# Two head groups per output bank, a rebuilt opening, another order of the steps and 118 dummy matmuls in a one-core transformer block

## The chip, the cores and the metric

The kernel runs on one core of a Trainium2 chip. The metric is the device time of one execution in microseconds (us); of several runs the median counts. The engines are named as in the profile: PE is TensorE, DVE is VectorE, ACT is ScalarE, POOL is GpSimd, SP issues DMAs.

## What is computed

`x` is 4 x 512 x 128 in fp32. It is normalised to `xn`, and the result is `x + local(xn) + ffn(xn)`. Cut to what matters:

```python
# local: attention in chunks of 16 tokens, once on neighbours, once on every third token; 16 heads of 8
local = linear(chunk_attention(xn, 16) + dilated_chunk_attention(xn, 16, 3), Wo, bo)

# ffn: causal attention over all 512 tokens, 16 heads, low-rank q, k, v and rotary parts
probs = softmax(where(causal, qq @ kk.T / sqrt(8), min))
y     = (probs @ v).reshape(B, S, 128) @ W_o
x     = xn + y
# then a shared expert and two of seven routed experts
h     = silu(xt @ Wg) * (xt @ Wu) @ Wd          # for each of 8
out   = x + shared + sum(weight_e * routed_e)
```

## The kernel before

The host only lays out data; everything else is one program for one core. Activations of a batch (512 tokens) are turned so that features lie on partitions. The program is a list of steps, `ORDER`, which every engine walks in the same order, each doing its own part of a step; engines meet only on semaphores. So a step's place in the list sets its place in every queue, SP's and POOL's too. The fields after a step's name are the batch, then the head group or unit.

**Steps.** The opening of a batch is `XT` (transposes of the normalised tokens: L1211), `LK`, `LQ`, `LV` (local projections: L1216, L1300), `MA` and `MB` (projections for the causal attention and their rotated forms: L1221), `MV` (its values: L1227), and `STATS`, `LN` (normalisation on VectorE). `WF` (L1200) multiplies low-rank weights, once. VectorE adds the rotary parts (L961, L992, L993, L995, L965) and splits q and k into bf16 terms, and SP writes the terms to the stacks in which the score products find them (steps `ST`, `to_stack`, L484). `KD` spreads k over `k_diag` for the local attention (L774 on ScalarE, L1003 on VectorE).

`S.b.n` are products of the causal attention whose maxima VectorE takes (L1159 on TensorE, L1012 on VectorE, banks A); `SHIFT` turns a group's maxima and SP writes them back into the q stack. `E` are the same products again, shifted by the maxima (L1180, banks B), of which ScalarE takes the exponent (L830). A `*` in `ORDER` stands for the next S with the E that lies two head groups behind; their matmuls alternate on TensorE. 176 of each run in all. `mask` adds the causal triangles (L1166).

`PV.b.g.j` multiplies probabilities of head group `g` and key tile `j` with values and a column of ones (L1276) into one bank, `bank_c`: each head of the group has 32 of its 128 partitions, of which 9 are used. After the last `j` ScalarE copies the bank to `oT_mla` (L839). `Y.b.g` transposes it back (four transposes, L1283), and VectorE divides by the sums (L1074, L1075) into `y_mla`. The next group's first PV waits for the copy:

```python
if j == 0 and n > 1:
    pe.wait_ge(c_drained, (n - 1) // NT)
...
first = (HD + 1) * (4 * g + m)
```

`YT` and `X1` finish the causal attention. `LS`, `LR`, `PT`, `LO`, `LT`, `LW` are the local attention (L1318; L1026 and L1029 on VectorE). `R2`, `R3`, `X2T`, `ROUTE`, `PICK` are the second normalisation and the routing. The last part of the list are 32 experts (4 batches by 8): `GU` (gate and up, L1372, banks B) and `DOWN` (L1378, banks A). The expert weights take the room of `k_diag`, so they come behind the last `LS`.

**Banks.** Eight PSUM banks: rings A (2; S, LS, DOWN), B (3; E, GU) and M (2; everything else), and `bank_c`. `wait_free` makes TensorE wait until the bank's last user was read. In a pair of S and E it waits for both banks before the first matmul of the pair.

**Dummies.** `WARM` gives steps a number of fp32 matmuls of the identity with itself into `bank_c`, issued ahead of the step's waits: 6 ahead of `WF`, 2 ahead of `XT.0.1`, 2 ahead of `MA.0.0`, 10 ahead of `S.0.0`, one ahead of each of `S.0.2` to `S.0.11` (L1192).

## Time and profile before

| | us |
|---|---|
| median of 3 timed runs | 378.18 |
| lowest and highest of them | 376.24, 379.63 |
| the profiled execution | 371.83 |
| its span, first to last instruction | 369.6 |
| PE, DVE, ACT, POOL busy | 334.2, 285.0, 222.3, 123.0 |

The profile is one execution. Busy times are sums over instructions; matmuls are pipelined and their ends modelled, so that PE may be listed as busy while the next matmul could already stream in. The name behind an arrow (`<-`) is what released a waiting engine. The granted clock is 1.00 at full speed and 0.50 at half. The profiled execution is shorter than each of the timed runs.

### The profile page before, as it was taken

Reading aid. Unit: us, or ns where it says so; the run is one execution under the profiler, and the core shown is the slowest. Engines: PE = TensorE matmul, PEld = TensorE weight load, DVE = VectorE, ACT = ScalarE, POOL = GpSimd, SP = SyncE. Lnnn points to the kernel's source line nnn. Section 1 sums busy time; section 2 is a strip of 40 time slices with the busy share of each in tenths; the row PEclk is TensorE's granted clock in tenths of the full one; section 3 lists DMA queues with packets and bytes.
Section 4 is the critical chain, followed back from the end, with each engine's and each line's share of the span. In section 5 each row is a group of like instructions: output and inputs, shape, how many; then the busy total and the mean of one; then the engine's idle time right before and its main releaser. Section 6 shows DMA issues by size and latency. Waiting matters only on the chain.

```text
span 369.6 us, 11664 instructions
## 1 busy us (share of the span) xinstructions
PE 334.2 (90%) x4504; PEld 206.3 (56%) x4504; DVE 285.0 (77%) x720; ACT 222.3 (60%) x545; POOL 123.0 (33%) x148
## 2 busy tenths in 40 slices
PE   5779997898998989999989899888999999999994
PEld 5455664455564555565654565534546666656663
DVE  5979789799877988898998988987334577766743
ACT  5266345577675656677674766665765656456563
POOL 6186507040600826603312200000203563444443
PEclk9999999999999989999998999989999999999998
DMA  8435352222242123250222321106000000000000
GB/s 200 77 108 173 71 167 62 67 62 42 40 162 46 36 66 51 78 184 25 43 53 50 65 65 34 36 3 172 5 0 0 3 27 2 4 28 2 29 0 28
DMA packets 29141, 21.84 MB, mean 59 GB/s; under 512 B 12312, under 2 KB 26008, under 8 KB 29048
## 3 DMA queue, kind: packets, MB, share of 16 engines
q1 hardware_dynamic: 28872, 20.91, 22.8%
q8 instruction: 36, 0.59, 0.7%
q10 hardware_dynamic: 216, 0.20, 0.2%
q14 instruction: 17, 0.14, 0.1%
HBM read 6.81 MB, written 6.19 MB: 35 GB/s over the span
## 4 chain that ended last, share of the span: by engine, by line
PE 60%; DVE 28%; issue 5%; ACT 3%; DMA 3%; SPq 1%; POOL 0%; DVEq 0%; ACTq 0%; POOLq 0%
PE bank_B L1372 13%; DVE neg_max L1012 9%; PE bank_B L1180 8%; PE bank_c L1276 7%; PE bank_A L1378 7%; PE bank_A L1318 3%; PE bank_M L1283 2%; PE bank_B L1166 2%; DVE s_loc L1029 2%; DVE row_max L1026 2%; PE bank_M L1341 2%; PE bank_M L1221 2%; PE bank_c L1192 2%; PE bank_M L1211 1%; PE bank_M L1326 1%
## 5 line engine op out<-in xcount | busy, mean ns | idle before, releaser
L830 ACT ACTIVATE p_mla<-bank_B 128x512 f32<-128x512 f32 (+1 forms) x176 | 92.0, 561 | 54.6 <-PE bank_B L1166 31.0
L1012 DVE TENSOR_REDUCE neg_max<-bank_A 128x1 f32<-128x512 f32 (+3 forms) x176 | 106.9, 636 | 15.8 <-PE bank_A L1166 13.0
L1180 PE MATMUL bank_B<-q_stack,k_stack 54*128 54x512 bf16 (+3 forms) x256 | 62.4, 306 | 12.1 <-DVE neg_max L1012 8.2
L1159 PE MATMUL bank_A<-k_stack,q_stack 52*128 52x512 bf16 (+3 forms) x256 | 63.1, 307 | 3.2 <-DMA q_stack<-parts 2.2
L1372 PE MATMUL bank_B<-xrT,k_diag 128*128 128x512 f32 x128 | 60.9, 597 | 1.1 <-DVE k_diag L1137 1.1
L703 POOL TENSOR_TENSOR x<-x,q_part 128x512 f32<-128x512 f32 x31 | 39.5, 1274 | 58.0 <-ACT q_part L864 41.7
L1276 PE MATMUL bank_c<-p_mla,v_mla 128*32 128x384 f32 (+12 forms) x512 | 47.6, 453 | 0.4 <-ACT p_mla L830 0.4
L1180 PEld LDWEIGHTS bank_B<-q_stack,k_stack 54*128 54x128 bf16 x256 | 19.4, 94 | 49.6 <-issue 23.4
L864 ACT ACTIVATE q_part<-bank_A,expert_w 128x128 f32<-128x128 f32 x108 | 30.8, 369 | 24.6 <-PE bank_A L1378 24.6
L1137 DVE SCALAR_TENSOR_TENSOR k_diag<-k_diag,bank_B 128x512 f32<-128x512 f32 x32 | 22.0, 687 | 29.1 <-ACT k_diag L848 26.7
L1166 PE MATMUL bank_A<-masks 64*128 64x64 bf16 (+2 forms) x352 | 43.9, 204 | 0.0
L1166 PE MATMUL bank_B<-masks 64*128 64x64 bf16 (+2 forms) x352 | 43.8, 204 | 0.0
L1378 PEld LDWEIGHTS bank_A<-k_diag 128*128 128x128 f32 x256 | 33.1, 191 | 14.1 <-issue 14.1
L1166 PEld LDWEIGHTS bank_B<-masks 64*128 64x128 bf16 x352 | 32.6, 97 | 12.8 <-issue 0.9
L609 POOL TENSOR_TENSOR nrm<-nrm,half 128x8 f32<-128x8 f32 (+1 forms) x8 | 10.7, 1332 | 73.4 <-DVE nrm L1088 65.1
L1378 PE MATMUL bank_A<-k_diag 128*128 128x128 f32 x256 | 33.9, 275 | 0.7 <-DVEq L1145 0.7
L1166 PEld LDWEIGHTS bank_A<-masks 64*128 64x128 bf16 x352 | 32.8, 97 | 1.8
L1372 PEld LDWEIGHTS bank_B<-xrT,k_diag 128*128 128x128 f32 x128 | 21.6, 191 | 18.0 <-issue 13.6
L1142 DVE TENSOR_TENSOR k_diag<-bank_B,k_diag 128x512 f32<-128x512 f32 x32 | 22.1, 691 | 1.1
L1159 PEld LDWEIGHTS bank_A<-k_stack,q_stack 52*128 52x128 bf16 x256 | 19.3, 94 | 6.3 <-issue 3.7
L848 ACT ACTIVATE k_diag<-bank_B 128x512 f32<-128x512 f32 x32 | 19.5, 610 | 3.6 <-PE bank_B L1372 3.6
L1318 PE MATMUL bank_A<-k_diag,q_part 128*32 128x128 f32 x544 | 20.1, 277 | 0.7 <-DVE neg_max L1012 0.7
(150 smaller groups left out, 550.4 us busy)
## 6 DMA issues: line engine op xcount, KB each, us to landing
v_dram<-v_rows SPq DMA_DIRECT2D x12, 324.0 KB, 3.8
k_stack<-parts SPq DMA_DIRECT2D x48, 64.0 KB
q_stack<-parts SPq DMA_DIRECT2D x45, 64.0 KB
k_diag<-k_part SPq DMA_DIRECT2D x48, 34.0 KB
v_diag<-v_dram SPq DMA_DIRECT2D x32, 45.0 KB, 2.1
v_diag<-v_dram SPq DMA_DIRECT2D x32, 36.0 KB, 1.9
v_dram<-v_rows SPq DMA_DIRECT2D x4, 283.5 KB, 2.8
x<-in_x SPq DMA_DIRECT2D x4, 256.0 KB, 7.8
```

The lines of the kernel that those rows point to most:

```text
L703: link(nc.gpsimd.tensor_tensor(x[:, tb, :], x[:, tb, :], weighted[down_no[step] % 2], ALU.add))
L830: drained_by(nc.scalar.activation(p_of(n)[:, m:m + len(heads), 0:w], src, ACT.Exp, scale=SCALE), step)
L864: ins = nc.scalar.activation(weighted[n % 2][:, i, :], down[:, i, :], ACT.Copy, scale=expert_w[:, c * NT + i, e - 1:e])
L1012: drained_by(nc.vector.tensor_reduce(neg_max[:, g, m:m + len(heads), i], src, AX.X, ALU.max, negate=True), step)
L1142: ins = nc.vector.tensor_tensor(hid[n % 2], bank_of(step + (1,))[:], hid[n % 2], ALU.mult)
L1159: return nc.tensor.matmul(bank_of(step)[:, n * w:(n + 1) * w], q_stack[b % 2][rows, h % 8, i * P:(i + 1) * P], k_stack[b % 2][rows, h % 8, ...
L1166: return nc.tensor.matmul(to, half_eye[half, low, :], triangle[half, :].unsqueeze(1).broadcast_to((SLOT, len(heads), SLOT)), start=False, ...
L1180: nc.tensor.matmul(bank_of(step)[:, m * w:(m + 1) * w], k_stack[b % 2][rows, h % 8, j * P:(j + 1) * P], q_stack[b % 2][rows, h % 8, j * P: ...
L1276: last = nc.tensor.matmul(bank_c[32 * m:32 * m + width, j * P:], heads[:, first:first + width], p_of(n)[:, m, 0:S - j * P], start=(j == 0) ...
L1318: last = nc.tensor.matmul(bank[PAIR * j:PAIR * j + PAIR, c:c + P], q_part[:, a, pair, :], k_diag[:, a, :, CHUNK * pair:CHUNK * pair + CHUN ...
L1372: full_by(nc.tensor.matmul(bank_of(use)[:], w_exp[:, e, m, :], x2T[:, c, :], start=True, stop=True), use)
L1378: last = nc.tensor.matmul(bank[:, i * D:(i + 1) * D], hid[n % 2][:, i * P:(i + 1) * P], w_exp[:, e, 2, :], start=True, stop=True)
```

## The change

**Two head groups per bank.** Groups 0 and 1 now share `bank_c`, and so do 2 and 3. `v_mla` gets 18 columns a head, nine zeros in front of the eight values and the one; the even group reads from the values on and the odd one from the zeros on, so that in the 32 partitions of a place the first group lands in rows 0 to 8 and the second in rows 9 to 17, each adding zeros to the other's. The heads are dealt out anew for it (group `g`, place `m` is head `4m + g`; `WF` on VectorE permutes the weights). ScalarE's copy and `Y` come once for two groups, 8 times in place of 16, and `Y` divides twice as many elements. The number of PV matmuls stays at 512.

```diff
-                elif kind == "PV" and step[3] == NT - 1:
+                elif kind == "PV" and step[3] == NT - 1 and step[2] % 2:
                     _, b, g, _ = step
                     act.wait_ge(pv_done, pv_no[step])
@@ PV on TensorE
-                    if j == 0 and n > 1:
-                        pe.wait_ge(c_drained, (n - 1) // NT)
+                    second = g % 2
+                    if j == 0 and not second and n > 1:
+                        pe.wait_ge(c_drained, (n - 1) // (2 * NT))
                     heads = v_mla[:, b % 2, j].rearrange("p h d -> p (h d)")
                     for m in range(4):
-                        first = (HD + 1) * (4 * g + m)
-                        width = min(PV_WIDTH, H * (HD + 1) - first)
+                        first = (HD + 1) * (2 * (4 * m + g) + 1 - second)
+                        width = min(PV_WIDTH, 2 * (HD + 1) * (H + 1) - first)
@@ Y on VectorE
-                        y_mla[:, :, 4 * HD * g:4 * HD * g + 4 * HD].rearrange("p i (h d) -> p i h d", h=4), o[:, :, :, 0:HD],
-                        den.unsqueeze(3).broadcast_to((P, NT, 4, HD)), ALU.mult), step)
+                        y_places[:, :, c:c + 2 * HD].rearrange("p n (a d) -> p n a d", a=2), o[:, :, :, 0:HD],
+                        den.unsqueeze(3).broadcast_to((P, H, 2, HD)), ALU.mult), step)
```

On TensorE, batch 0, behind the first group's last PV, there stood a Y and then the next group's PV (`oT_mla` is the copied output bank, `p_mla` the probabilities):

```order
L1283 MATMUL bank_M<-eye,oT_mla 128x128 x4
L1276 MATMUL bank_c<-p_mla,v_mla 32x512 x4
L1326 MATMUL bank_M<-eye,p_loc 128x64 x2
L1180 MATMUL bank_B<-q_stack,k_stack 128x384
L1159 MATMUL bank_A<-k_stack,q_stack 128x384
```

Now the second group's first PV stands there without one:

```order
L1403 MATMUL bank_M<-eye,p_loc 128x64 x2
L1352 MATMUL bank_c<-p_mla,v_mla 32x512 x4
L1427 MATMUL bank_M<-eye,y_loc 128x128 x2
L1243 MATMUL bank_B<-q_stack,k_stack 128x384
L1222 MATMUL bank_A<-k_stack,q_stack 128x384
```

The four transposes (and with them a wait for ScalarE's copy) come only behind the second group.

**Opening.** ScalarE adds the two bias tails and does half of `k_part` of batch 0 (`k_halves`), POOL the memsets of `s_loc` and of the larger `v_mla`; both were VectorE's or POOL's alone. `XT.0.0`, `MA.0.1`, `LK.0`, `LQ.0` and `MV.0` use the B banks (`EARLY_IN_B`). The dummies on the identity are other ones; the single ones ahead of `S.0.2` to `S.0.11` are gone:

```diff
-WARM = {("WF",): 6, ("XT", 0, 1): 2, ("MA", 0, 0): 2, ("S", 0, 0): 10, **{("S", 0, n): 1 for n in range(2, 12)}}
+WARM = {("LV", 0, 0): 16, ("LV", 0, 1): 6, ("MA", 0, 0): 5, ("MA", 0, 1): 3, ("MB", 0): 16, ("S", 0, 0): 10, ("WF",): 14, ("XT", 0, 0): 3, ("XT", 0, 1): 8}
```

On TensorE the opening up to the projections of the local attention stood so (`eye` with itself is a dummy, `lat_room` is WF, `w_mla` are MA and MB):

```order
L1192 MATMUL bank_c<-eye 128x128 x6
L1200 MATMUL bank_M<-lat_room 128x64 x3
L1200 MATMUL bank_M<-lat_room 128x128
L1192 MATMUL bank_c<-eye 128x128 x2
L1211 MATMUL bank_M<-eye,xr 128x128 x4
L1192 MATMUL bank_c<-eye 128x128 x2
L1221 MATMUL bank_M<-xrT,w_mla 128x512 x3
L1211 MATMUL bank_M<-eye,xn 128x128 x4
L1216 MATMUL bank_M<-xnT,wide 128x512 x2
```

and now:

```order
L1255 MATMUL bank_c<-eye 128x128 x14
L1264 MATMUL bank_M<-lat_room 128x64 x3
L1264 MATMUL bank_M<-lat_room 128x128
L1255 MATMUL bank_c<-eye 128x128 x8
L1275 MATMUL bank_M<-eye,xr 128x128 x4
L1255 MATMUL bank_c<-eye 128x128 x5
L1285 MATMUL bank_M<-xrT,w_mla 128x512
L1255 MATMUL bank_c<-eye 128x128 x16
L1285 MATMUL bank_M<-xrT,w_mla 128x512
L1291 MATMUL bank_B<-w_mla_v,xrT 128x128 x4
L1255 MATMUL bank_c<-eye 128x128 x3
L1275 MATMUL bank_B<-eye,xn 128x128 x4
```

The second and third product with `w_mla` (MB.0 and MA.0.1) are no longer next to the first. Behind these rows come 3 dummies, MA.0.1, LK, LQ, 16 dummies, LV.0.0, 6 dummies, LV.0.1, LV.0.2 and 10 dummies, and then the first score product; before, LV.0.1 and LV.0.2 stood behind it.

On VectorE the chain from these products to the stacks had nothing in between:

```order
L961 TENSOR_TENSOR rot<-bank_M,rope 128x512
L992 TENSOR_TENSOR p_loc<-bank_M,rope 64x512
L993 TENSOR_TENSOR rot<-rot,p_loc 64x512
L995 TENSOR_TENSOR turned_q<-bank_M,rope 64x512
L961 TENSOR_TENSOR rot<-bank_M,rope 128x512
L965 TENSOR_TENSOR rot<-rot,turned_q 64x512
```

Now the statistics of batch 1 (`STATS.1`) stand in its middle:

```order
L1014 TENSOR_TENSOR rot<-bank_M,rope 128x512
L1045 TENSOR_TENSOR p_loc<-bank_M,rope 64x512
L1046 TENSOR_TENSOR rot<-rot,p_loc 64x512
L1048 TENSOR_TENSOR turned_q<-bank_M,rope 64x512
L939 BN_STATS stats<-x 128x6 x4
L942 BN_AGGR mv<-stats 128x2 x4
L945 TENSOR_SCALAR nrm<-mv 128x4
L946 RECIPROCAL nrm<-nrm 128x4
L947 TENSOR_TENSOR nrm<-mv,nrm 128x4
L1014 TENSOR_TENSOR rot<-bank_B,rope 128x512
L1018 TENSOR_TENSOR rot<-rot,turned_q 64x512
```

**Order.** All of `ORDER` is replaced. Two lines of it, before and now:

```diff
-LN.0 WF XT.0.1 MA.0.0 MB.0 MA.0.1 XT.0.0 ST.0.0 LK.0 LQ.0 STATS.1 ST2.0 MV.0 ROOT LV.0.0 KD.0.0 * KD.0.1 * KD.0.2
+LN.0 WF XT.0.1 MA.0.0 MB.0 STATS.1 MV.0 XT.0.0 MA.0.1 LK.0 LQ.0 ST.0.0 LV.0.0 LV.0.1 LV.0.2 VD.0.0 ROOT STATS.2
```

**Fills.** A table `FILLS` names 34 steps (31 E, 3 S) with 1 to 8 dummies each, 118 in all: bf16 products of the mask tables, 128 x 192. In a pair, TensorE now waits for E's bank, runs the dummies into it, and then waits for S's bank:

```diff
+            def fill(step, to):
+
+                for _ in range(FILL.get(step, 0)):
+                    nc.tensor.matmul(to[:, 0:FILL_WIDTH], masks[:, 0:P], masks[:, 0:FILL_WIDTH], start=True,
+                                     stop=True, skip_group_check=True)
@@ E on TensorE
                     other = beside.get(step)
+                    if other:
+                        wait_free(pe, step)
+                        fill(step, bank)
+                        wait_free(pe, other)
+                    else:
+                        if step in FILL:
+                            wait_free(pe, next_down[step])
+                            fill(step, bank_of(next_down[step]))
+                        wait_free(pe, step)
```

By batch the dummies are 36, 20, 29 and 33; the batches' E steps with dummies are 9, 4, 10 and 8.

## Rows read from the trace of the kernel before

**Rows 1.** Page, part 1: busy time, share of the span, instructions of TensorE.

```profile
PE 334.2 (90%) x4504; PEld 206.3 (56%) x4504; DVE 285.0 (77%) x720; ACT 222.3 (60%) x545; POOL 123.0 (33%) x148
```

**Rows 2.** Windows: busy us by engine (instructions), granted clock, DMA share, GB/s.

```profile
33.00:66.00 33.00, 29.38 (x530) 18.94 (x532) 28.63 (x58) 14.38 (x37) 15.73 (x20) 0.95 0.42 119
66.00:273.70 207.70, 190.63 (x3366) 112.84 (x3358) 171.01 (x443) 136.82 (x333) 46.65 (x67) 0.97 0.26 61
273.70:369.60 95.90, 89.97 (x441) 57.13 (x440) 59.78 (x133) 52.99 (x152) 41.80 (x33) 0.98 0.04 12
```

**Rows 3.** Timeline in a stretch of paired score steps: start us, us, engine line.

```profile
74.93 1.96 DVE L1012 TENSOR_REDUCE neg_max<-bank_A 128x1 f32<-128x512 f32 x3
75.68 0.39 PE L1180 MATMUL bank_B<-q_stack,k_stack 54*128 54x512 bf16 x1 [0.26 <-DVE neg_max L1012]
```

**Rows 4.** Lines: busy us, mean ns | idle us before, by what ended it.

```profile
L1180 PE MATMUL bank_B<-q_stack,k_stack 54*128 54x512 bf16 (+3 forms) x256 | 62.4, 306 | 12.1 <-DVE neg_max L1012 8.2 <-DMA q_stack<-shift 1.2 <-DVE s_loc L1029 1.0
L1283 PE MATMUL bank_M<-eye,oT_mla 128*128 128x128 f32 x64 | 11.2, 301 | 1.4 <-DVE y_loc L1043 0.8 <-ACT oT_mla L839 0.5
L1074 DVE RECIPROCAL rden_mla<-bank_M 128x16 f32<-128x16 f32 x16 | 4.0, 252 | 8.2 <-PE bank_M L1283 8.0
L1075 DVE TENSOR_TENSOR lat_room<-bank_M,rden_mla 128x128 f32<-128x128 f32 x16 | 4.7, 292 | 0.6
L1166 PEld LDWEIGHTS bank_B<-masks 64*128 64x128 bf16 x352 | 32.6, 97 | 12.8 <-issue 0.9
```

**Rows 5.** Chain that ended last, expert part: start us, us, what.

```profile
350.57 1.72 PE bank_B L1372 x4
352.29 0.89 PE bank_A L1378 x8
```

**Rows 6.** Cores: span and mean granted clock.

```profile
core 0: 369.6 us, clock 0.978
```

**Rows 7.** Windows of 2 us, columns as in rows 2.

```profile
60.00:62.00 2.00, 0.86 (x12) 0.43 (x12) 1.82 (x4) 0.60 (x1) 1.86 (x3) 1.00 0.35 96
64.00:66.00 2.00, 2.00 (x69) 1.20 (x62) 1.54 (x5) 0.94 (x3) 0.00 (x0) 0.50 0.29 88
196.00:198.00 2.00, 1.98 (x18) 1.43 (x18) 1.63 (x6) 0.49 (x1) 0.00 (x0) 0.50 0.03 5
```

**Rows 8.** Timeline of the opening: start us, us, engine, line, operation.

```profile
3.90 2.90 PE L1192 MATMUL bank_c<-eye 128*128 128x128 f32 x12 [3.90 <-DMA eye<-in_c_eye]
...
6.73 2.07 PE L1200 MATMUL bank_M<-lat_room 32*128 32x64 f32 x8
...
11.74 3.08 PE L1221 MATMUL bank_M<-xrT,w_mla 128*128 128x512 f32 x6
...
13.73 0.68 DVE L992 TENSOR_TENSOR p_loc<-bank_M,rope 64x512 f32<-64x512 f32 x1
...
15.89 0.69 DVE L961 TENSOR_TENSOR rot<-bank_M,rope 128x512 f32<-128x512 f32 x1
...
20.25 0.96 DVE L976 TENSOR_TENSOR parts<-p_loc,parts 128x512 bf16<-128x512 f32 x1
...
21.14 0.86 DVE L885 BATCH_NORM_STATS2 stats<-x 128x6 f32<-128x128 f32 x4
...
21.32 2.50 PE L1192 MATMUL bank_c<-eye 128*128 128x128 f32 x20
...
22.86 0.28 DVE L893 TENSOR_TENSOR nrm<-mv,nrm 128x4 f32<-128x4 f32 x1
...
24.46 6.50 ACT L774 ACTIVATE k_diag<-k_part,head_mask 128x544 f32<-128x544 f32 x10
...
26.06 0.37 PE L1159 MATMUL bank_A<-k_stack,q_stack 52*128 52x512 bf16 x1 [2.24 <-DMA q_stack<-parts]
...
41.84 0.69 DVE L1026 TENSOR_REDUCE row_max<-bank_A 128x32 f32<-128x512 f32 x1 [0.35 <-PE bank_A L1318]
...
60.75 0.60 ACT L830 ACTIVATE p_mla<-bank_B 128x512 f32<-128x512 f32 x1 [1.27 <-PE bank_B L1166]
```

More of the change, by code:

```diff
@@ L217, in bank_uses @@
         return [("A", step)]
-    if kind == "E":
+    if kind == "E" or step in EARLY_IN_B:
         return [("B", step)]
@@ L292, in build @@
     waits_for_e = set(beside.values())
+    next_down, ahead = {}, None
+    for step in reversed(steps):
+        ahead = step if step[0] == "DOWN" else ahead
+        next_down[step] = ahead
     with ExitStack() as ctx:
@@ L756, in _ @@
                     drain(step, kT[:, 0:S], bank[:], bias=cols[:, 1:2])
+                    if b == 0:
+                        wait_drained(act, step)
+                        act.wait_ge(v_rows_set, 1)
+                        for par in range(2):
+                            for dst, src in k_halves(1, par):
+                                ins = nc.scalar.copy(dst, src)
+                        ins.then_inc(k_part_by_act, 1)
+                        act.wait_ge(rest_ready, 1)
+                        nc.scalar.copy(parts[:, 0, 1, :], rest[:]).then_inc(rounded[0], 1)
                 elif kind == "LV":
@@ L1192, in _ @@
                     nc.tensor.matmul(bank_c[:, 0:P], eye[:], eye[:], start=True, stop=True)
-                if step in where and kind != "SHIFT":
-                    wait_free(pe, step)
+                if step in where:
                     bank = bank_of(step)
+                    if kind not in ("S", "E", "SHIFT"):
+                        wait_free(pe, step)
                 if kind == "WF":
@@ L1237, in _ @@
                     if step not in waits_for_e:
+                        fill(step, bank_c)
+                        wait_free(pe, step)
                         for n in range(len(UNITS[step[2]][1])):
```

181 lines of the change are left out of this document (112 added, 69 removed).

## Prediction

> **What bounds the kernel now.** I read the page's busy shares first. TensorE is busy 90% of the span [rows 1], which suggests that matmuls are the limit. The windows by stage say something finer [rows 2]: in the score part (33 to 273.7 us) TensorE is busy 190.6 of 207.7 us in the long stretch and VectorE 171.0, while in the expert part (95.9 us) VectorE has room and TensorE is busy for 90. The timeline of a paired score step [rows 3] shows who sets the pace: three maxima on VectorE take 1.96 us, 0.65 each, and the next pair on TensorE starts only 0.26 us after it could, released by that maximum. A matmul that is listed as busy for 0.39 us is mostly pipeline, so the 90% is not a full engine. The line view agrees: ahead of the exponents' matmuls (L1180) TensorE sat idle for 12.1 us, 8.2 of it until VectorE had freed a bank [rows 4]. So in the score part VectorE and the order of its work lead, with TensorE close behind; in the expert part it is TensorE alone, 1.72 + 0.89 = 2.61 us for each of 32 experts, back to back in the chain [rows 5].
>
> The third limit is the clock. The mean granted clock was 0.978 [rows 6], a loss of 0.022 x 369.6 = 8.1 us of full-speed time. The windows show it as short stretches at 0.50, that is 1.2 in place of 2.4 GHz; ahead of the first TensorE was busy for only 0.86 of 2 us [rows 7]. By rows 2 the losses are 33.0 x 0.05 = 1.7 and 207.7 x 0.03 = 6.2 in the score part (rounded clocks, so 6 to 8 together) and 95.9 x 0.02 = 1.9 in the expert part.
>
> The profiled execution took 371.83 us: 369.6 of span and 2.2 around it. The median of the timed runs is 378.18, 6.35 more. I make the sum against the profiled one and carry it over to the median; the only term I let grow there is the clock, because of all that these rows show it is what most likely differs between executions.
>
> **The change part by part.**
>
> *Opening.* TensorE's dummies on the identity ahead of the first score matmul go from 20 to 81. In the trace six took 2.90 us at the start, 0.48 each, and ten took 2.50 us later, 0.25 each [rows 8]: the two levels of the clock. Ahead of MB.0 there are now 43 where there were 10. The old ten lay behind a load and two drains. The new ones don't fit there: 14 slow ones are 6.7 us and 29 fast ones 7.3, so from 3.90 MB.0 starts at 3.9 + 14.0 + 2.1 (WF) + 0.7 (four transposes, as in a Y [rows 4]) + 1.0 (MA.0.0) = 21.7, where it started behind MA.0.0 at about 12.8 (a product takes a third of the 3.08 us). If the clock rises early and all are fast it is 17.4. So MB.0 is 4.6 to 8.9 us late, and VectorE's chain for the stacks (13.73 to 21.21) with it. That chain also gets STATS.1 in its middle, 21.14 to 23.14 in the old trace, about 2 us, and in the same time TensorE has MV, XT.0.0 and six dummies ahead of MA.0.1, some 2.2 us more than the old 15.89 - 13.73. The memsets and tails that leave VectorE for POOL and ScalarE give nothing here, since they ended as the first product did. The chain's end to the first maximum was 26.06 - 21.21 = 4.85 us and stays; so by the chain the first maximum comes at 26.06 + (4.6 to 8.9) + 2.2 = 33 to 37. On TensorE itself LK, LQ, three LVs and 32 more dummies (8.0 us) stand in that time, about as long as the chain needs, and may add 2. I take 36, 10 us late.
>
> Not all of it stays. The old opening did LN.1, STATS.2, two of VectorE's four k_diag products and two LVs behind the first maximum; now they stand ahead of it. From 36 the next mark, the second local maximum (41.84 before), needs eleven maxima at 0.7 and one local step of 1.4, or ScalarE's twelve k_diag copies (ten took 6.50 us, so 7.8) behind the last LV: about 47. I take +5 us, with +1 (fast clock, everything caught up) and +10 (nothing caught up) as bounds.
>
> *Two head groups per bank.* Eight of 16 Y steps go. A Y is 11.2/16 = 0.70 us on TensorE and 0.25 + 0.29 on VectorE [rows 4]; the eight that stay read twice as much on VectorE, so it saves 8 x 0.54 less the extra elements. Nothing shows a Y of that size. If it costs double, VectorE saves nothing; if it costs the same, 4.3 us. The PV matmuls keep their number and width. If TensorE led everywhere, all 5.6 would come back; I take 3.5, bounds 1 and 6. Eight copies of the output bank leave ScalarE; they count as nothing, since its work is hidden behind the other two.
>
> *118 dummies at 34 steps* (the table names 34). Each is a bf16 product of 192 columns with a load of 128. The trace has no such shape. The nearest rows are the loads of the mask, 0.097 us each [rows 4], and the 512-column product, 0.39 with its pipeline [rows 3]: 118 x 0.097 = 11.4 us and 118 x 0.39 = 46. Laid back to back on one bank, I take 0.1. The idle time ahead of L1180 is 12.1 us, so 11.8 nearly fill it. Behind a dummy wait its pair and every step after it, since TensorE is in order; what overshoots goes to VectorE as a late maximum. I take +1, bounds 0 and +6.
>
> What do they buy? If short waits let the clock fall, filled waits hold it. In the profiled execution I let them take back 4 of the 6 to 8 us in the score part, and 2 more of the 6.35 that the median lies above it: -6 on the median. Bounds: -12 and +2 (four of the 34 steps lie in batch 1, so a stretch there may well stay).
>
> The Trainium skill ("TensorE: Matmul & The Clock Gate", section "A second HAM failure mode: psum-queue depth-cycling") describes this case: small waits between groups that cycle through PSUM banks make the clock oscillate. The trace agrees, with 0.86 of 2 us busy ahead of a stretch at 0.50; taken fully, the rule gives the third rival below. Another rule speaks against the dummies (same page, Part 3, "The mechanism"): a weight load overlaps running matmuls only in another row group. The pairs use one half of the rows each, the dummies all of them, so by that rule each of the 34 places pays a load in and a load out, 34 x 0.2 = 6.8 us in place of my 1, and the time would be 376.0.
>
> *The order.* All 352 score steps, PV and local steps stand in another order, with fewer steps of the M banks and of ScalarE to fit. TensorE's idle time from 66 to 273.7 is 17.1 us and VectorE's 36.7 [rows 2]; I give the order a fifth of TensorE's, -3.5. Bounds: -8 (half) and +5 (as much lost again as a third of it). The ten single dummies ahead of early maxima are replaced by nine small ones: nothing, as VectorE leads there.
>
> *Expert part.* Its 32 x 2.61 = 83.5 us stay. The other 12.4 us of the stretch are routing, normalisation and the last projection; RMS and routing of batch 2 now start earlier: -1, bounds -3 and +2.
>
> Sum on the profiled execution: +5 - 3.5 + 1 - 4 - 3.5 - 1 = -6, 365.8 us. On the median, with 2 more for the clock: 378.2 - 8 = **370.2 us**.
>
> **Rivals.** Faster or slower counts here beyond 1% (below 374.4, above 382.0), about what a measurement of this kernel can tell from no change.
>
> 1. *The opening decides (slower).* Its place is MB.0 behind 43 dummies, its price the full 10 us. It decides if the first paired exponent, at 60.75 before [rows 8], is over 8 us late: then VectorE's maxima, which lead up to the last of them, never catch up. For it: VectorE is busy 28.6 of 33 us from 33 to 66. Against: some 5 us of its work is moved ahead. With Y and overshoot as above, half of the clock's gain, and nothing from the order and the expert part: 378.2 + 10 - 3.5 + 1 - 3 = 382.7; with overshoot at its bound 388.
>
> 2. *The freed time is hidden (no change).* If VectorE leads throughout and a Y of double size costs double, the merge gives 1, the order nothing, the clock 3 because a slow TensorE mostly waited anyway: 378.2 + 5 - 1 + 1 - 3 - 1 = 379.2.
>
> 3. *The clock holds throughout (much faster).* The dummies and the dense opening keep it at 2.4 GHz in every execution: the 6.35 of the median and 5 in the score part both go. 378.2 + 5 - 3.5 + 1 - 11.4 - 3.5 - 1 = 364.8; with an opening of +1, 361. For it: the slow stretches follow waits. Against: 34 places are few beside 176 pairs.
>
> **How the numbers follow.** The forecast gets 0.44, rival 1 0.20, rival 2 0.16, rival 3 0.20. The forecast's own range is 365 to 376, and of its 0.44 I put 0.38 below 374.4; with rival 3 that is 0.58 for faster. Rival 2 and the forecast's upper end give 0.20 for the same, rival 1 and the tail of rival 2 0.22 for slower. The range reaches down to rival 3 with its cheap opening and a little below, 358, and up to rival 1 between its two prices, 386.
>
> **What would show it.** Right: the first maximum at 33 to 39 us, MB.0's product at 17 to 22; the second local maximum near 47; a mean granted clock above 0.985; eight Y steps, each under 0.8 us on VectorE; idle time ahead of the paired exponents well below 12.1 us; an expert stretch of 94 to 96 us. Wrong: a first maximum before 30 us (the dummies cost less than rows 8 say), or a clock at 0.978 or lower with all dummies in place (then it isn't the short waits that lower it), or a score part that ends over 5 us later than 273.7.

## The result, and the profile after

| | before | after |
|---|---|---|
| median, us (20 runs each) | 375.56 | 377.22 |
| lowest and highest | 370.41, 381.72 | 373.71, 379.62 |
| the profiled execution | 371.83 | 375.88 |
| its span | 369.6 | 374.0 |

The ratio of after to before is 1.0092, 95% interval [1.0056, 1.0128]: no gain, and a loss at the edge of what was called no change. This ratio, like those below, leaves out disturbed runs, most of them of the kernel before, which the medians keep, so it is higher than that of the two medians, 377.22 / 375.56 = 1.0044. 370.2 was forecast.

The page's busy shares and the core view of after, which answer to [rows 1, 6]:

```profile
PE 348.1 (93%) x4692; PEld 221.1 (59%) x4692; DVE 281.3 (75%) x700; ACT 222.6 (60%) x543; POOL 124.0 (33%) x147
```

```profile
core 0: 374.0 us, clock 0.994
```

TensorE has 13.9 us more to do, VectorE 3.7 less, and the clock is nearly full. By [rows 6] a clock of 0.978 cost 8.1 us; 0.994 costs 0.006 x 374.0 = 2.2. So by this estimate about 6 us of clock were won, where 4 were forecast for the profiled execution, and its span is 4.4 us longer all the same: some 10 us have gone elsewhere. (Over its 20 runs after has a mean clock of 0.985, so this execution is one of the better ones.) The windows, with the columns of [rows 2]:

```profile
0.00:33.00 33.00, 29.15 (x257) 25.92 (x258) 23.15 (x86) 13.45 (x21) 16.20 (x20) 1.00 0.36 99
33.00:66.00 33.00, 29.35 (x470) 18.45 (x469) 25.42 (x47) 18.87 (x43) 15.70 (x24) 1.00 0.44 129
66.00:273.70 207.70, 194.31 (x3458) 116.42 (x3457) 174.44 (x437) 133.29 (x320) 50.22 (x72) 0.99 0.27 64
```

From 33 to 66 us VectorE does 25.42 us of work where it did 28.63. The matching hole lies ahead of it, in the timeline of the opening, which answers to [rows 8]:

```profile
3.85 5.26 PE L1255 MATMUL bank_c<-eye 128*128 128x128 f32 x28 [3.85 <-DMA eye<-in_c_eye]
...
13.56 1.02 PE L1285 MATMUL bank_M<-xrT,w_mla 128*128 128x512 f32 x2
...
14.42 3.73 PE L1255 MATMUL bank_c<-eye 128*128 128x128 f32 x32
...
14.69 0.69 DVE L1014 TENSOR_TENSOR rot<-bank_M,rope 128x512 f32<-128x512 f32 x1 [1.33 <-PE bank_M L1285]
...
17.99 1.02 PE L1285 MATMUL bank_M<-xrT,w_mla 128*128 128x512 f32 x2
...
19.05 0.69 DVE L1045 TENSOR_TENSOR p_loc<-bank_M,rope 64x512 f32<-64x512 f32 x1 [3.67 <-PE bank_M L1285]
...
21.22 0.87 DVE L939 BATCH_NORM_STATS2 stats<-x 128x6 f32<-128x128 f32 x4
...
24.09 3.73 PE L1255 MATMUL bank_c<-eye 128*128 128x128 f32 x32
...
33.97 0.39 PE L1222 MATMUL bank_A<-k_stack,q_stack 52*128 52x512 bf16 x1
...
34.45 1.29 DVE L1065 TENSOR_REDUCE neg_max<-bank_A 128x1 f32<-128x512 f32 x2 [0.34 <-PE bank_A L1229]
...
46.20 0.69 DVE L1079 TENSOR_REDUCE row_max<-bank_A 128x32 f32<-128x512 f32 x1 [0.35 <-PE bank_A L1395]
...
62.64 0.60 ACT L884 ACTIVATE p_mla<-bank_B 128x512 f32<-128x512 f32 x1 [4.01 <-PE bank_B L1229]
```

One row says most: `p_loc` waits 3.67 us for MB.0, and MB.0 (17.99) stands behind 16 dummies (14.42, 3.73 us; a count of two is one dummy, so 0.233 each). TensorE's own queue became as long as VectorE's chain: the first maximum (34.45) waits the last 0.34 us for TensorE's product, which stands right behind dummies. The first score product comes at 33.97 where it came at 26.06, 7.9 late; the second local maximum at 46.20, 4.4 late; the first exponent at 62.64, 1.9 late.

The line view, answering to [rows 4]:

```profile
L1243 PE MATMUL bank_B<-q_stack,k_stack 54*128 54x512 bf16 (+3 forms) x256 | 62.6, 302 | 9.4 <-DVE neg_max L1065 3.6 <-DMA q_stack<-shift 2.1 <-issue 1.1
...
L1215 PE MATMUL bank_B<-masks 128*128 128x192 bf16 x107 | 13.9, 249 | 0.0
...
L1360 PE MATMUL bank_M<-eye,oT_mla 128*128 128x128 f32 x32 | 5.1, 282 | 0.2 <-ACT oT_mla L893 0.2
...
L1132 DVE TENSOR_TENSOR lat_room<-bank_M,rden_mla 128x256 f32<-128x256 f32 x8 | 3.4, 424 | 0.3
...
L1130 DVE RECIPROCAL rden_mla<-bank_M 128x32 f32<-128x32 f32 x8 | 2.8, 350 | 0.9 <-PE bank_M L1360 0.7 <-DVE k_diag L1199 0.2
```

The fills did fill: TensorE's idle time behind VectorE's maxima ahead of the exponents' products is 3.6 us, from 8.2 (and 9.4 in run 2, which is after without fills). Y became cheap: eight of 0.350 + 0.424 = 0.77 us on VectorE, 6.2 in all from 8.7, and 5.1 on TensorE from 11.2. The experts run as before, 1.72 and 0.89 us in the chain [rows 5].

### The profile page after: what moved, and what is told of

Same layout as the page of the kernel before. It is cut to its first block, busy times and chain, and to the rows that moved or that the text cites. A ratio compares the mean times of both kernels' runs of the same rounds, so it can differ in the third digit from the quotient of the medians.

```text
span 374.0 us, 11968 instructions
## 1 busy us (share of the span) xinstructions
PE 348.1 (93%) x4692; PEld 221.1 (59%) x4692; DVE 281.3 (75%) x700; ACT 222.6 (60%) x543; POOL 124.0 (33%) x147
## 4 chain that ended last, share of the span: by engine, by line
PE 77%; DVE 11%; ACT 5%; issue 4%; DMA 1%; SPq 1%; POOL 0%; DVEq 0%; ACTq 0%; POOLq 0%
PE bank_B L1449 15%; PE bank_B L1243 11%; PE bank_c L1352 9%; PE bank_A L1455 7%; PE bank_c L1255 5%; PE bank_A L1395 4%; DVE neg_max L1065 3%; PE bank_B L1229 3%; PE bank_B L1215 3%; PE bank_M L1418 2%; PE bank_M L1285 2%; PE bank_M L1377 2%; ACT k_diag L828 2%; PE bank_M L1403 2%; PE bank_M L1280 1%
## 5 line engine op out<-in xcount | busy, mean ns | idle before, releaser
L884 ACT ACTIVATE p_mla<-bank_B 128x512 f32<-128x512 f32 (+1 forms) x176 | 94.1, 560 | 66.1 <-PE bank_B L1229 48.3
L1065 DVE TENSOR_REDUCE neg_max<-bank_A 128x1 f32<-128x512 f32 (+3 forms) x176 | 108.2, 637 | 18.2 <-PE bank_A L1229 15.2
L1352 PE MATMUL bank_c<-p_mla,v_mla 128*32 128x128 f32 (+3 forms) x512 | 46.8, 447 | 1.1 <-ACT p_mla L884 1.1
L1455 PEld LDWEIGHTS bank_A<-k_diag 128*128 128x128 f32 x256 | 33.1, 191 | 14.0 <-issue 13.9
L1255 PE MATMUL bank_c<-eye 128*128 128x128 f32 x162 | 21.8, 294 | 3.8 <-DMA eye<-in_c_eye 3.8
L1255 PEld LDWEIGHTS bank_c<-eye 128*128 128x128 f32 x162 | 20.8, 208 | 5.3 <-issue 5.2
```

The lines of the kernel that those rows point to most:

```text
L884: drained_by(nc.scalar.activation(p_of(n)[:, m:m + len(heads), 0:w], src, ACT.Exp, scale=SCALE), step)
L1065: drained_by(nc.vector.tensor_reduce(neg_max[:, g, m:m + len(heads), i], src, AX.X, ALU.max, negate=True), step)
L1255: nc.tensor.matmul(bank_c[:, 0:P], eye[:], eye[:], start=True, stop=True)
L1352: last = nc.tensor.matmul(bank_c[32 * m:32 * m + width, j * P:], heads[:, first:first + width], p_of(n)[:, m, 0:S - j * P], start=(j == 0 ...
L1455: last = nc.tensor.matmul(bank[:, i * D:(i + 1) * D], hid[n % 2][:, i * P:(i + 1) * P], w_exp[:, e, 2, :], start=True, stop=True)
```

## The experiments

The clock differs from run to run, so each experiment below has its mean granted clock beside its time. The 71 runs of the kernel before that were made beside the experiments show what it is worth: 369.8 to 385.3 us at clocks of 0.985 to 0.94, and a straight line through them, 376.0 us at 0.9675 and 3.1 us less for each 0.01 more (correlation -0.92). After's own 20 runs give 2.8 us for each 0.01. "At equal clock" means the mean distance from that line; above a clock of 0.985, where the line's runs end, it is an extrapolation. For after it is +6.6 us, at a mean clock of 0.985. "By the ratios" means the difference of two ratios to the kernel before, in us of its time.

**Runs 1 and 2. Which half costs, the opening's dummies or the fills.** Run 1 is after with only before's 20 dummies in the opening:

```diff
-WARM = {("LV", 0, 0): 16, ("LV", 0, 1): 6, ("MA", 0, 0): 5, ("MA", 0, 1): 3, ("MB", 0): 16, ("S", 0, 0): 10, ("WF",): 14, ("XT", 0, 0): 3, ("XT", 0, 1): 8}
+WARM = {("WF",): 6, ("XT", 0, 1): 2, ("MA", 0, 0): 2, ("S", 0, 0): 10}
```

> The changed kernel with the opening's identity dummies of the kernel before: 20 in place of 81 (6, 2, 2 and 10). Opening theory (the 61 more dummies stand on the path to the first maximum): the first maximum comes near 27 us instead of 34.45, the second local maximum near 40 to 42 instead of 46.2, and the time falls by 4 to 7 us, to 370 to 373, below the kernel before. Rival (VectorE's work, not the start, sets the score part, so that a late start is caught up): within 1 us of the changed kernel. Rival (the dummies pay by keeping the clock up): clock below 0.975 in most runs and no gain.

Measured: 368.71 us (367.63 to 369.12), clock 0.988, before beside it 375.19, ratio 0.9872 [0.9806, 0.9939]. The same kernel again, in five rounds (below: run 1 again):

> The changed kernel with the 20 old opening dummies once more, in more rounds, to bound its gain over the kernel before: 367.5 to 370, ratio 0.978 to 0.988, clock 0.983 to 0.991, if the first four runs were typical; 371 to 374 if they were lucky in where the low stretches fell.

369.25 us, ratio 0.9889 [0.9838, 0.994], clock 0.985, which is the clock of after too: so at one and the same clock the 61 added dummies cost 377.22 - 369.25 = 8.0 us (7.6 to 8.2 by the ratios). The timeline of run 1 shows `p_loc` without a wait, a wait of TensorE for ScalarE ahead of LV.0.2, and the first maximum 4.4 us earlier than in after (2.8 in the profiled execution of run 1 again, where it came at 31.63):

```profile
15.69 0.68 DVE L1045 TENSOR_TENSOR p_loc<-bank_M,rope 64x512 f32<-64x512 f32 x1
...
25.32 0.64 PE L1377 MATMUL bank_M<-wide,xnT 128*32 128x128 f32 x4 [3.58 <-ACT v_rows L778]
...
30.07 2.11 DVE L1065 TENSOR_REDUCE neg_max<-bank_A 128x1 f32<-128x512 f32 x3
```

Run 2 is after without the fills:

```diff
-FILLS = {
...
-}
+FILLS = {}
```

> The changed kernel without its 118 small dummies. Cost theory (each of the 34 places delays its pair and what stands behind it, as the rule on weight loads in other row groups says): 2 to 6 us faster, with the clock hardly lower. Clock theory (the fills hold the clock): mean clock 0.970 or lower where it was 0.983 to 0.986 in most runs, and 3 to 5 us slower. Rival (they lie in idle time and do nothing): within 1 us and the same clock.

378.66 us, ratio 1.0128 [1.005, 1.0206], clock 0.973. With the heavy opening in place the fills are worth only 378.66 - 377.22 = 1.4 us.

**Runs 3 and 4. Without both, and then in before's order.** Run 3 has both edits:

> Both edits together: 20 identity dummies in the opening and no fills, so that only the two head groups per bank, the moved opening work and the new order are left. If opening and fills each cost what their theories say, the gains add up: 366 to 370 us. If the new order and the merged Y give nothing by themselves, the time is that of the kernel before, 374 to 377. If both kinds of dummies paid through the clock, it is slower than the changed kernel.

373.70 us, ratio 0.9987 [0.9932, 1.0042], clock 0.965. Against run 1 the fills are worth 5.0 us here (4.3 by the ratios). By the line they cost 2.2 us at equal clock and bring 0.0225 of clock.

Runs 2 and 3 also give the price of the 61 dummies without fills: 5.0 us by the medians, while the clock goes from 0.965 to 0.973. At equal clock it is 7.4 us (from -3.4 to +4.0), much as with the fills, 7.8 (from -1.2 to +6.6). So dummies and fills both raise the clock, but it can be won only once: behind the heavy opening the fills bring 1.4 us and not 5.0, because the clock was up already.

Run 4 is the same kernel with the steps in before's order:

```diff
-ORDER = """
-LN.0 WF XT.0.1 MA.0.0 MB.0 STATS.1 MV.0 XT.0.0 MA.0.1 LK.0 LQ.0 ST.0.0 LV.0.0 LV.0.1 LV.0.2 VD.0.0 ROOT STATS.2
...
+ORDER = """
+LN.0 WF XT.0.1 MA.0.0 MB.0 MA.0.1 XT.0.0 ST.0.0 LK.0 LQ.0 STATS.1 ST2.0 MV.0 ROOT LV.0.0 KD.0.0 * KD.0.1 * KD.0.2
...
```

> As the run before it, but with the order of the kernel before, in which the Y steps of head groups 0 and 2 are left out. What is left of the change is the merge and the moved opening work. Merge theory (each Y that goes frees 0.4 us of path): 3 to 6 us faster than the kernel before, 370 to 373. Hidden theory (VectorE and ScalarE's waits lead, the merge frees only covered time): within 1.5 us of the kernel before. Against the run before it, it tells what the new order is worth: as fast or faster means that the order gave nothing, slower by 3 or more that the order is the gain.

373.81 us, ratio 1.0031 [0.9993, 1.007], clock 0.965. The new order by itself is worth 0.1 us, at the same clock (1.6 by the ratios, whose intervals overlap).

**Runs 5 and 6. The fills elsewhere.** Run 5 is run 4 with the fills:

> The merge and the moved opening work in the order of the kernel before (without its eight Y steps), with the 20 opening dummies and the 118 fills at the same steps. The run with the new order and the same dummies took 368.71. If the fills work at any place where a pair waits, this one comes within 1.5 us of it, with a clock of 0.98 or more against 0.964 without fills. If the fills were worth something only where the new order waits, the clock stays near 0.965 to 0.975 and the time at 371 to 374: then the gain of the order is that it goes with its fills.

383.33 us at a mean clock of 0.967, in four runs that differ widely: 378.35 us at 0.980, 382.28 at 0.970, 384.38 and 385.96 at 0.959. The median lies 9.5 us above run 4, and even the fastest lies 3.7 above run 4's slowest, 374.66. Whether the fills raised the clock, four such runs don't say. Run 6 is the kernel before itself with the 109 fills at the E steps (the three S steps have the other nine of the 118; the 115 of the expectations is a slip), and E's bank waited for ahead of S's, as after does:

```diff
+                    if other:
+                        wait_free(pe, step)
+                        fill(step, bank)
+                        wait_free(pe, other)
```

> The kernel before with the new wait order in a pair and the 31 fills ahead of exponents (115 dummies); its own dummies stay. In 20 runs of the kernel before, time and clock lie on a line of 3.1 us per 0.01 of clock. Clock theory: the clock rises from 0.967 to 0.98 or more and the time falls by 2 to 4 us, to 371 to 373. Cost theory: what the clock gives the dummies take back, 374 to 377. Against the run with merge, old order and fills it gives the merge by itself: 3 us at equal clock by the line.

380.16 us, ratio 1.0174 [1.0075, 1.0273]. Here the clock does rise, to 0.984, and the time with it, to 9.6 us above the line. The wait order alone isn't the cause, as run 4 has it too and no fills. So the fills are no good in themselves: it takes the order that was made with them.

**Run 7. The places by a single step.** It is run 1, but each of the 109 fills at E steps stands at the next E step:

```diff
-FILLS = {
-    1: """
-    E.0.0.1.1 E.0.1.0.2 E.0.3.0.0 E.2.0.0.1 E.2.0.0.3 E.2.2.3.0 E.2.3.0.1 E.3.0.3.0 E.3.2.1.1 E.3.3.1.1 S.0.1
...
+FILL = {('E', 0, 0, 1, 2): 1, ('E', 0, 1, 0, 3): 1, ('E', 0, 3, 0, 1): 1, ...
```

> The changed kernel with the 20 old opening dummies and the same 118 fills, the 115 ahead of exponents each one exponent step later. In place it took 368.71 with a clock of 0.988. Place theory (fills cost nothing only at the steps where TensorE waits for a bank anyway, which is why the same table cost 9 us in the old order): 372 to 378, and the clock no better than 0.98. Rival (any pair waits, so any place will do, and the old order failed for another reason): within 1.5 us of 368.7.

373.28 us, ratio 0.9979 [0.994, 1.0018], clock 0.986. One step later the same fills give back 4.0 to 4.6 us, about all that they had brought, at the clock of run 1 again (0.985). So the clock stays won, and the time is lost to waits. The two lines that show how (line numbers shift a little), first without fills, run 3:

```profile
L1040 DVE TENSOR_REDUCE neg_max<-bank_A 128x1 f32<-128x512 f32 (+3 forms) x176 | 107.5, 636 | 18.4 <-PE bank_A L1204 15.1
...
L1218 PE MATMUL bank_B<-q_stack,k_stack 54*128 54x512 bf16 (+3 forms) x256 | 62.5, 304 | 15.0 <-DVE neg_max L1040 9.7 <-DVE s_loc L1059 1.7 <-DMA q_stack<-shift 1.4
```

Then run 1, and run 7:

```profile
L1065 DVE TENSOR_REDUCE neg_max<-bank_A 128x1 f32<-128x512 f32 (+3 forms) x176 | 108.0, 636 | 16.3 <-PE bank_A L1229 13.1
...
L1243 PE MATMUL bank_B<-q_stack,k_stack 54*128 54x512 bf16 (+3 forms) x256 | 62.0, 300 | 8.4 <-DVE neg_max L1065 3.9 <-DMA q_stack<-shift 1.1 <-DVE s_loc L1084 1.0
```

```profile
L1039 DVE TENSOR_REDUCE neg_max<-bank_A 128x1 f32<-128x512 f32 (+3 forms) x176 | 107.7, 636 | 18.0 <-PE bank_A L1203 15.0
...
L1217 PE MATMUL bank_B<-q_stack,k_stack 54*128 54x512 bf16 (+3 forms) x256 | 62.5, 304 | 10.1 <-DVE neg_max L1039 5.7 <-DMA q_stack<-shift 1.7 <-DVE s_loc L1058 1.5
```

And in before's order, run 4 without fills and run 5 with them:

```profile
L1041 DVE TENSOR_REDUCE neg_max<-bank_A 128x1 f32<-128x512 f32 (+3 forms) x176 | 107.4, 636 | 17.0 <-PE bank_A L1205 13.7
...
L1219 PE MATMUL bank_B<-q_stack,k_stack 54*128 54x512 bf16 (+3 forms) x256 | 62.2, 302 | 14.8 <-DVE neg_max L1041 10.9 <-DVE s_loc L1060 1.5 <-DMA q_stack<-shift 0.5
```

```profile
L1066 DVE TENSOR_REDUCE neg_max<-bank_A 128x1 f32<-128x512 f32 (+3 forms) x176 | 107.9, 636 | 22.7 <-PE bank_A L1230 19.9
...
L1244 PE MATMUL bank_B<-q_stack,k_stack 54*128 54x512 bf16 (+3 forms) x256 | 63.0, 305 | 11.9 <-DVE neg_max L1066 9.1 <-DMA q_stack<-shift 1.0 <-DVE s_loc L1085 0.6
```

In place, the fills stand where TensorE waited: its waits for maxima fall from 9.7 us to 3.9, and VectorE's maxima wait less for TensorE as well, 13.1 us in place of 15.1. One step later TensorE still waits 5.7 us, and the maxima 15.0, as long as without fills. In before's order the fills hardly meet a wait (10.9 us, then 9.1), and the maxima wait in turn for TensorE: 19.9 us in place of 13.7. Each pair is one execution of each kernel.

**Run 8. Two head groups per bank alone.** Before with the merge, and with it the tails on ScalarE and two memsets on POOL; its order, opening and dummies stay.

```diff
-                elif kind == "PV" and step[3] == NT - 1:
+                elif kind == "PV" and step[3] == NT - 1 and step[2] % 2:
```

> The kernel before with the two head groups per bank alone: its own order (without eight Y), its own opening, banks and identity dummies; only the memsets and bias tails that the larger value tile brings stay moved. Merge theory (the term of 3.5 us was right, and the moved opening work is what took some of it back): first maximum at 26 to 27 us, 3 to 5 us faster than the kernel before at equal clock (line of 40 runs of before: 376.4 us at 0.966, 3.25 us per 0.01), so 371 to 374 near 0.966. Hidden theory: within 1.5 us of that line.

373.57 us, before beside it 373.62, ratio 0.9952 [0.99, 1.0004], clock 0.976, and +0.3 us at equal clock: at most 1%, and not told apart from nothing. The first maximum came at 28.89 us, later than the 26 to 27 expected. The beginning shows part of it, before and then run 8:

```profile
8.22 1.12 DVE L946 TENSOR_SCALAR xr<-x,mv,nrm 128x128 f32<-128x128 f32 x4
```

```profile
7.88 2.16 POOL L648 MEMSET v_mla<- 128x2448 f32 x1
...
8.42 2.28 DVE L967 TENSOR_SCALAR xr<-x,mv,nrm 128x128 f32<-128x128 f32 x4
```

While POOL clears the larger `v_mla`, the same four VectorE instructions take 2.28 us in place of 1.12, and XT.0.1, which reads `xr`, starts at 10.76 in place of 9.74. All kernels here with this memset have 2.28 or 2.29; run 6, which like before has none at that time, has 1.11. No run moved the memset alone.

**Runs 9 and 10. Parts of the opening, taken away.** Run 9 is after without MB.0's sixteen dummies:

```diff
-("MA", 0, 1): 3, ("MB", 0): 16, ("S", 0, 0): 10
+("MA", 0, 1): 3, ("S", 0, 0): 10
```

> The changed kernel without the 16 dummies ahead of MB.0 alone; the other 65 stay. Path theory (these stand between the two products on which VectorE's chain waits, 16 x 0.23 = 3.7 us): first maximum near 31 to 32 in place of 34.45 and 3 to 4 us faster, 373 to 374. Rival (TensorE's own queue of dummies behind them, 32 ahead of the first maximum, is the longer path, so that any 16 count alike): also 3 to 4 us faster, but TensorE idle ahead of the first maximum stays under 0.5 us. Rival (the stacks' DMA is what is waited for): under 1.5 us faster, and TensorE waits over 2 us for the DMA ahead of the first maximum.

376.66 us, ratio 1.0092 [1.004, 1.0144], where after has 377.22: a miss, although the first maximum came as expected. Run 10 is run 1 with STATS.1 moved out of VectorE's chain:

```diff
-LN.0 WF XT.0.1 MA.0.0 MB.0 STATS.1 MV.0 XT.0.0 MA.0.1 LK.0 LQ.0 ST.0.0
+LN.0 WF XT.0.1 MA.0.0 MB.0 MV.0 XT.0.0 MA.0.1 LK.0 LQ.0 STATS.1 ST.0.0
```

> The changed kernel with the 20 old opening dummies (368.71), and with STATS.1 put back behind LQ.0, where the kernel before has it, so that VectorE's chain to the stacks isn't interrupted. If the 2 us of STATS.1 lie on the path: first maximum near 28 in place of 30.1, and 1 to 2 us faster, 367 to 368. If the chain waits for MA.0.1 anyway, which has MV and XT.0.0 ahead of it: first maximum at 29.5 to 30.1 and within 0.7 us.

373.57 us, ratio 1.0013 [0.9944, 1.0083], clock 0.975, where run 1 again has 369.25: a miss again, and in the wrong direction. Its timeline shows why nothing could be won:

```profile
28.89 0.37 PE L1222 MATMUL bank_A<-k_stack,q_stack 52*128 52x512 bf16 x1 [1.23 <-DMA q_stack<-parts]
...
32.96 1.27 DVE L1065 TENSOR_REDUCE neg_max<-bank_A 128x1 f32<-128x512 f32 x2
...
33.18 1.09 PE L1275 MATMUL bank_M<-eye,xn 128*128 128x128 f32 x4 [3.29 <-DVE xn L1005]
```

The first score product did come earlier (28.89; run 1 has 29.47), but its maximum came only at 32.96, since VectorE works without a pause up to there: STATS.1 now stands behind the chain, and still ahead of the first maximum, with STATS.2, the `k_diag` products and LN.1. TensorE waits 3.29 us for LN.1 meanwhile. The windows add the clock (each is one execution, of run 10 the slowest of ten). Run 9, then run 10, with the columns of [rows 2]:

```profile
30.00:40.00 10.00, 8.10 (x82) 5.58 (x81) 6.04 (x14) 7.68 (x13) 8.79 (x12) 0.85 0.52 161
40.00:50.00 10.00, 10.00 (x92) 5.49 (x92) 5.50 (x9) 3.55 (x10) 3.73 (x8) 0.63 0.35 94
```

```profile
30.00:40.00 10.00, 6.60 (x55) 4.15 (x59) 6.99 (x16) 5.10 (x9) 8.15 (x12) 0.51 0.41 120
40.00:50.00 10.00, 10.00 (x71) 5.29 (x64) 5.35 (x8) 2.71 (x8) 3.75 (x8) 0.50 0.26 71
```

Through the first steps TensorE ran at half speed, for a part of the time in run 9 and for nearly all of it in run 10. In run 9 the first maximum stood at 31.75 us, 2.7 earlier than in after, and the mean clock over its ten runs is 0.979, where after has 0.985. At equal clock it lies at +4.0 where after lies at +6.6: by the line 2.6 us were won by the place, and most of it was lost by the clock. What such a run says of MB.0 is therefore unclear, and runs 12 to 15 were made for it.

**Run 11. Dummies only where TensorE waits anyway.** Run 1 with 39 in place of 20, 14 of them ahead of LV.0.2, where TensorE waited for 3.58 us:

```diff
+WARM = {("WF",): 6, ("XT", 0, 1): 5, ("MA", 0, 0): 2, ("LV", 0, 2): 14, ("S", 0, 0): 12}
```

> The changed kernel with its 118 fills and 39 identity dummies in the opening, put where the run with the old 20 showed TensorE waiting: 5 ahead of XT.0.1 (0.79 us of wait), 14 ahead of LV.0.2 (3.58 us of wait for ScalarE) and 12 ahead of the first maximum; none ahead of MB.0. If dummies cost only where TensorE has work and pay through the clock: first maximum at 28 to 30 us, no low stretch before 45 us, 367 to 369 with a clock of 0.985 or more, as fast as the run with the old 20 or up to 2 us faster. If any dummy in the opening costs its 0.23 us: 371 to 373.

368.79 us (365.95 to 369.85), ratio 0.9869 [0.9812, 0.9926], clock 0.993. Nineteen more dummies cost nothing here, and the clock is 0.005 to 0.008 above that of run 1.

**Runs 12 to 15. One group of dummies at a time.** On the ground of run 11, which holds its clock: run 12 is run 11 once more, run 13 adds the changed kernel's 16 ahead of MB.0, run 14 its 22 ahead of LV.0.0 and LV.0.1, run 15 has its early ones.

```diff
+("MB", 0): 16
...
+("LV", 0, 0): 16, ("LV", 0, 1): 6
...
+("WF",): 14, ("XT", 0, 0): 3, ("XT", 0, 1): 8, ("MA", 0, 0): 5, ("MA", 0, 1): 3
```

> The kernel with dummies in the opening's waits once more, as the ground for the three others on this chip: 368 to 370 us by all theories, clock above 0.985.

> The kernel with dummies in the opening's waits plus the changed kernel's 16 dummies ahead of MB.0. Theory (place decides: sixteen ahead of a product that VectorE waits for cost their whole 16 x 0.233 = 3.7 us): p_loc waits 3 to 4 us on MB.0, the first maximum comes 3 to 4 us later than 29.1, and the time is 3 to 4 us above the kernel without them, at 372 to 373. Rival (number decides: 8.5 us over 61 dummies are 0.14 each wherever they stand): 2.2 us above. Rival (the clock pays): a denser opening gives back what it costs, 0 to 1 us above.

> The same kernel plus the changed kernel's 16 dummies ahead of LV.0.0 and 6 ahead of LV.0.1, in place of MB.0's. Theory: 22 x 0.233 = 5.1 us of TensorE time stand behind VectorE's way to the stacks but ahead of k_diag's v rows and of the first score product; TensorE had 20.72 to 24.35 full of dummies already, so 3 to 5 us come on top, and the first maximum and the end are 2 to 4 us late. Rival (number decides): 3.1 us. Rival (only MB.0 counts): 0 to 1 us.

> The same kernel with the changed kernel's early dummies (14 ahead of WF, 8 ahead of XT.0.1, 5 ahead of MA.0.0, 3 each ahead of XT.0.0 and MA.0.1) and its own late ones. Theory: the first five places cost what MA.0.0 starts later, 13.56 against 12.74, and the six around XT.0.0 and MA.0.1 another 1.4 where VectorE has STATS.1 to do: 0.5 to 2 us above the kernel without. Rival (number decides): 20 more are 2.8 us. Rival (the clock rises earlier): equal or 1 us below.

| run | median us | ratio to before | clock | above run 12 | by the ratios |
|---|---|---|---|---|---|
| 12 | 367.93 | 0.9812 [0.9756, 0.9869] | 0.994 | | |
| 13, MB.0 | 374.85 | 0.9967 [0.9896, 1.0038] | 0.990 | 6.9 | 5.8 |
| 14, LV | 372.16 | 0.9913 [0.9845, 0.998] | 0.991 | 4.2 | 3.8 |
| 15, early | 371.19 | 0.9887 [0.9831, 0.9943] | 0.995 | 3.3 | 2.8 |

Five runs each. That the number of dummies decides is out: MB.0's sixteen cost 5.8 to 6.9 us (in the latter 0.004 less clock, 1.2 us by the line, is contained), nineteen in waits nothing. By the medians all three groups cost more than expected, MB.0's by far the most. They add up to 14.4 us (12.4 by the ratios), where after lies 9.3 above run 12; after lacks 16 dummies that run 12 has ahead of LV.0.2 and S.0.0, 3.7 us of TensorE. The groups also lengthen different paths: in run 13 the first maximum follows VectorE's own work without a wait, and in run 14 it waits 3.77 us for TensorE. The timelines and windows of runs 11 and 13 show the first group plainly, as their profiled clocks are 0.999 and 0.997. Run 11:

```profile
14.73 0.68 DVE L1045 TENSOR_TENSOR p_loc<-bank_M,rope 64x512 f32<-64x512 f32 x1
...
29.12 1.96 DVE L1065 TENSOR_REDUCE neg_max<-bank_A 128x1 f32<-128x512 f32 x3
```

```profile
29.10:257.00 227.90, 213.44 (x3847) 129.45 (x3848) 195.16 (x467) 145.02 (x352) 64.62 (x95) 1.00 0.29 72
257.00:364.10 107.10, 102.18 (x575) 63.78 (x575) 61.88 (x146) 61.02 (x168) 42.14 (x34) 1.00 0.04 11
```

Run 13:

```profile
13.70 3.73 PE L1255 MATMUL bank_c<-eye 128*128 128x128 f32 x32
...
18.33 0.68 DVE L1045 TENSOR_TENSOR p_loc<-bank_M,rope 64x512 f32<-64x512 f32 x1 [3.67 <-PE bank_M L1285]
...
32.74 1.96 DVE L1065 TENSOR_REDUCE neg_max<-bank_A 128x1 f32<-128x512 f32 x3
```

```profile
32.70:262.00 229.30, 213.22 (x3846) 129.51 (x3847) 194.95 (x467) 144.84 (x352) 64.38 (x95) 1.00 0.29 72
262.00:369.20 107.20, 102.25 (x576) 63.85 (x575) 61.98 (x146) 60.95 (x168) 42.19 (x34) 0.99 0.04 11
```

3.6 us of `p_loc`'s delay arrive whole at the first maximum. The score part behind it has the same instructions (but for one record) and busy times within 0.25 us on every engine, and takes 229.3 us, not 227.9; the rest takes 107.2, not 107.1. Of this delay ahead of the first maximum nothing is caught up, and 1.4 us come on top.

Run 12, the kernel of run 11 once more, gives a second case: in its profiled execution MA.0.0 and MB.0 took 3.75 us in place of 1.96 (granted clock 0.66 from 10 to 20 us), `p_loc` and the first maximum (31.20) came 1.8 and 2.1 us late, and the span was 366.1 us, 2.0 longer. There too nothing was caught up, but nothing came on top either.

## Why the prediction was wrong

Two kinds of steps failed: the opening, which it put too low, and two gains that were not there. The terms beside what the medians and the ratios gave; the runs of before beside run 4 had 375.19:

| term | forecast | by the medians | by the ratios | from |
|---|---|---|---|---|
| opening | +5 | +8.0 | +7.6 to +8.2 | after and run 1, twice; the 61 dummies alone |
| two head groups | -3.5 | -1.4 | +1.2 | run 4 and before; with the moved opening |
| order | -3.5 | -0.1 | -1.6 | runs 3 and 4 |
| overshoot of the fills, clock | +1 - 6 = -5 | -5.0 | -4.3 | runs 1 and 3 |
| expert part | -1 | -1.1 | | see below; part of the others |

With the two runs the other way round (2 and 3, then after and 2) the dummies cost 5.0 and the fills bring 1.4. At equal clock the terms come apart: the dummies cost 7.4 to 7.8 where +5 was forecast, the fills 2.2 to 2.6 where +1 was, and the clock went from 0.965 to 0.985, 6.2 us by the line, where 6 was. So it is the opening that was too low.

*The opening.* Its mechanism was right and so were its marks: MB.0 at 17.4 if all dummies are fast (17.99), the first maximum at 33 to 37 (34.45), the second local maximum near 47 (46.20). The step that failed is "Not all of it stays". Work that before did behind the first maximum was moved ahead of it, and I took this as 5 us caught up. At the second local maximum it does look so, 4.4 us late. But the reference for a delay is the same kernel without the dummies, run 1: there the rebuilt opening has its second local maximum at 41.6 and its end at 366.9, after at 46.2 and 374.0, so 4.6 us late first and 7.1 at the end (4.3 and 7.0 against run 1 again). The delay grows through the score part. Runs 11 and 13 show the same in small, 3.6 and then 5.1; runs 11 and 12, with 2.1 and then 2.0, don't. Why it grows is open: the fills sit where TensorE waited in an opening of one particular length, and a later start may move the waits away from them, but no run tried that by itself.

*The order.* Here the step was "I give the order a fifth of TensorE's" idle time, -3.5. It had no row behind it but the size of the idle time. Alone the order gives 0.1 us by the medians and 1.6 by the ratios. It isn't useless: the fills bring 4.3 to 5.0 us with it (run 1 against 3) and lose at least 3.7, by the medians 9.5, without it (run 5 against 4). It is made for the fills; two terms that I added are one.

*Two head groups.* Y's size was read right: under 0.8 us on VectorE, eight of them. But run 8 gives a ratio of 0.9952, at most 3.7 us by its interval, and run 4 with the moved opening one of 1.0031. VectorE saves 2.5 us and TensorE 6.1; little of it reaches the end. The step in question is "I take 3.5", out of the 5.6 that were to come back "if TensorE led everywhere". Run 4 is 1.4 us better than before by the medians and 3.3 at equal clock, which is not what the ratio says; so the size was most likely put too high, and by how much of the 3.5 stays open. The memsets that went to POOL with it, which the prediction put at nothing, delay XT.0.1 by 1.0 us where no dummies cover it (run 8).

*Fills and clock.* Their sum was right, and for a reason near the one given: 2.2 us of cost at equal clock, within 0 to +6, and a clock of 0.988 from 0.965. The forecast price of a dummy was not: in place they cost little because they replace a wait, out of place (run 5) they cost 9.5 us by the medians, beyond my bound. The rule that small waits between groups of products that cycle through PSUM banks make the clock oscillate (the Trainium skill, "TensorE: Matmul & The Clock Gate", section "A second HAM failure mode: psum-queue depth-cycling") agrees with runs 1 and 3, where the clock goes from 0.965 to 0.988 as the fills take the waits. It doesn't give the time: in runs 6 and 7 the clock rose too, to 0.984 and 0.986, with no gain. Whether a load of all rows in between costs 0.2 us at each place, as the prediction weighed, no run tells apart from the waits.

*Expert part.* From the last S step's product to the end it was 369.6 - 257.6 = 112.0 us and is 374.0 - 263.1 = 110.9. One of the signs of being wrong came, a score part that ends over 5 us later than 273.7: the last S product is 5.5 us late, and the last E product starts at 282.7 where it started at 273.3, in part because the new order puts the first experts ahead of it.

*The rivals.* What happened is the first rival's place with the forecast's clock: MB.0 behind dummies, 8 us for good, and 5 us back from fills and clock. Its condition was a first exponent over 8 us late; it came 1.9 us late (4.6 against run 1), and the opening decided all the same, so that point of decision was wrong. The third rival's clock nearly came, 0.985 on average over after's runs, with no gain to show for it. One reading of the prediction is off without touching the sum: a product listed with 0.39 us isn't mostly pipeline, as the next starts 0.22 us behind it (33.97 and 34.19 in after).

## What to carry to other kernels

Put dummy matmuls only where the engine waits in the trace, and ahead of nothing that another engine waits for: sixteen of 0.233 us ahead of one product cost 5.8 to 6.9 us, nineteen in waits cost nothing. A table of fills belongs to one order; after any edit ahead of them, read the waits again, as one step's shift lost nearly all of the gain. A clock that one edit has won can't be won again by the next. The versions of runs 1 and 11 beat both kernels, at 367.9 to 369.3 us: each was timed twice, and of the four ratios, 0.9812 to 0.9889, no interval reaches above 0.994.
